# Sums and division of the value products: once per batch, turned by products with a 128x36 selection matrix in place of 128x128 transposes

## The reference, cut to what matters

```python
scores = einsum('bhnd,bhmd->bhnm', q, k) / sqrt(D)
aw = softmax(scores)
topk = 12
kth = top_k(aw, topk)[0][..., -1:]
aws = aw * (aw >= kth)
aws = aws / (aws.sum(-1) + 1e-08)
o_s = einsum('bhnm,bhmd->bhnd', aws, v)
o_l = einsum(qf, kv) / (z + 1e-06)
o = (a * o_s + (1 - a) * o_l).reshape(B, N, C)
return o @ Wproj.T + bproj
```

## Time and profile before

| what | value |
|---|---|
| median of 3 runs | 1333.5 us (1332.71 to 1335.28) |
| span of the profiled execution, first to last instruction | 1331.1 us |
| median less that span | 2.4 us |
| busy share: PE, PEld, DVE, ACT, POOL | 78%, 52%, 95%, 86%, 83% |
| chain that ended last, by engine | DVE 57%, issue 33%, DVEq 6%, all others 3% |
| mean granted TensorE clock over the span | 0.930 |

### The profile page before, as it was taken

One profiled execution on the slowest core, in us unless ns is written; L12 is line 12 of the kernel. 1 busy time (PEld: TensorE's weight loads), 2 busy tenths in 40 slices (PEclk: granted clock), 3 DMA queues, 4 the chain that ended last, 5 costly groups with the idle time before them and its releaser, 6 DMA issues.

```text
span 1331.1 us, 40027 instructions
## 1 busy us (share of the span) xinstructions
PE 1040.0 (78%) x8964; PEld 693.5 (52%) x8964; DVE 1260.1 (95%) x4916; ACT 1138.5 (86%) x3978; POOL 1110.9 (83%) x1458
## 2 busy tenths in 40 slices
PE   3787877778787878877888787777877788787776
PEld 1455555555455555555555455554555555555544
DVE  5799999999999999999999999999999999999995
ACT  3689998989899888989989899888989888898885
POOL 4588898979789888888879889798888888889874
PEclk9989999989899798998989989898998998989998
DMA  2222222112222122221112221112221212221210
GB/s 57 72 59 63 77 77 75 35 57 64 77 76 72 29 64 65 76 77 47 53 53 76 77 76 46 55 57 71 76 76 35 66 53 76 77 76 33 64 49 13
DMA packets 165131, 82.31 MB, mean 62 GB/s; under 512 B 7747, under 2 KB 164933, under 8 KB 164934
## 3 DMA queue, kind: packets, MB, share of 16 engines
q1 hardware_dynamic: 164934, 80.54, 20.9%
HBM read 42.77 MB, written 37.75 MB: 60 GB/s over the span
## 4 chain that ended last, share of the span: by engine, by line
DVE 57%; issue 33%; DVEq 6%; ACT 1%; POOL 1%; PE 1%; DMA 0%; SPq 0%; POOLq 0%
DVE rest L525 21%; DVE top L518 21%; DVE next L531 8%; DVEq L72 5%; DVE drop L615 2%; DVE o_sparse L574 1%; ACT e L719 1%; DVE den L566 1%; DVE k_sum L593 1%; DVE stats L582 0%; PE work_ps L910 0%; PE work_ps L911 0%; DVE x_mv L588 0%; DVE d_max L557 0%; DVE den L571 0%
## 5 line engine op out<-in xcount | busy, mean ns | idle before, releaser
L386 POOL TENSOR_SCALAR below<-e,next 128x256 bf16<-128x256 f32 x768 | 696.1, 922 | 21.5 <-DVE next L531 21.3
L719 ACT ACTIVATE e<-score_ps,drop 128x256 f32<-128x256 f32 x1024 | 472.4, 480 | 108.2 <-DVE drop L615 105.5
L838 PE MATMUL turn_ps<-ident,e 128*128 128x128 f32 x2048 | 429.9, 303 | 10.9 <-ACT kept L685 10.4
L525 DVE MATCH_REPLACE8 rest<-e 128x256 f32<-128x256 f32 x1024 | 413.3, 404 | 0.0
L531 DVE MAX8 next<-rest 128x8 f32<-128x256 f32 x1024 | 407.5, 408 | 0.0
L839 PE MATMUL turn_ps<-minus_huge,below 128*128 128x128 bf16 x2048 | 402.5, 232 | 0.0
L518 DVE MAX8 top<-score_ps 128x8 f32<-128x256 f32 x1024 | 359.4, 410 | 41.8 <-issue 21.7
L838 PEld LDWEIGHTS turn_ps<-ident,e 128*128 128x128 f32 x2048 | 312.2, 152 | 80.9 <-ACT kept L685 17.9
L685 ACT ACTIVATE kept<-turn_ps 128x512 f32<-128x512 f32 x512 | 285.1, 620 | 33.8 <-PE turn_ps L839 14.3
L839 PEld LDWEIGHTS turn_ps<-minus_huge,below 128*128 128x128 bf16 x2048 | 234.5, 115 | 0.0
L719 ACT ACTIVATION_READ_ACCUMULATOR e<-score_ps,drop 128x1 f32 x1024 | 217.1, 212 | 0.0
(11 more groups left out here) (141 smaller groups left out, 1540.6 us busy)
## 6 DMA issues: line engine op xcount, KB each, us to landing
part_slots<-part SPq DMA_DIRECT2D x128, 192.0 KB, 2.3
q_slots<-part_slots SPq DMA_DIRECT2D x64, 256.0 KB, 3.4
k_slots<-part_slots SPq DMA_DIRECT2D x64, 256.0 KB, 4.1
part_slots<-part SPq DMA_DIRECT2D x64, 128.0 KB, 1.9
x_sb<-in_L_attn_x SPq DMA_DIRECT2D x32, 128.0 KB, 3.6
x_res<-in_L_attn_x SPq DMA_DIRECT2D x32, 128.0 KB, 3.7
out_y<-out_sb SPq DMA_DIRECT2D x32, 128.0 KB, 4.2
w_ops<-in_L_ffn_W SPq DMA_DIRECT2D x1, 512.0 KB
```

The costliest lines, as they stand in the source:

```text
L386: nc.gpsimd.tensor_scalar(below[:, r, t, :], e[:, r, t, :], next8[:, r, t, TOPK - 9:TOPK - 8], None, ALU.is_lt).then_inc(s["below_pool"], 1)
L525: nc.vector.match_replace(rest[:, t, :], e8[:, (u_ - 1) % 2, t, :], e[:, (u_ - 1) % RING, t, :], REMOVED).then_inc(s["rest_ready"], 1)
L719: nc.scalar.activation(e[:, u_ % RING, t, :], score_ps[:, u_ % 2, t // 2, t % 2, :], ACT.Exp, bias=drop[:, u_ % 2, t, 0:1], accum_out=z[:, ...
L838: mm(dst, e[:, r, t, keys], ident[:], start=True, stop=False, is_transpose=True)
```

## The change

The transposes of `sums` become products with `heads_of`, a matrix of 128 rows by 4 x 9 columns of zeros and ones that GpSimd makes once at the start: column (j, e) picks partition 32 j + e. A product of a 128x128 block of `oT` (the weights) with it has 36 columns and no gaps, so the two halves of the rows, 2 x 4 x 36 = 288 columns, fit into `pv_ps` (512 columns) together. `sums` now makes all eight products in unit 5, and nothing in unit 7. VectorE works on both halves with one `den` (32 columns in place of 16), one reciprocal and one `o_sparse` (256 columns in place of 128), all in unit 5 at the same places k = 1, 2 and 4. `product` waits in unit 6 for the whole of `o_sparse`, and no longer in unit 0. The arithmetic is the same.

```diff
+        heads_of = sb("heads_of", [P, 4, VA])
...
-        den = sb("den", [P, 2, NT, H])
+        den = sb("den", [P, 2, NT * H])
...
+            nc.gpsimd.memset(heads_of[:], 0.0).then_inc(s["pool_step"], 1)
+            select(heads_of[:], ALU.not_equal, 1.0, 0, [[-VW, 4], [-1, VA]], 1, 7).then_inc(s["pool_const"], 1)
...
-                        pool.wait_ge(s["osp_ready"], NT * (it - 1))
+                        pool.wait_ge(s["osp_ready"], it - 1)
...
-                    if u_ in (5, 7) and 1 <= k <= 4 and exists(it - 1):
-                        t = (u_ - 5) // 2
-                        w = pv_ps[:].rearrange("p (h e) -> p h e", e=VW)
-                        n = 2 * (NT * (it - 1) + t)
+                    if u_ == 5 and 1 <= k <= 4 and exists(it - 1):
+                        w = pv_ps[:, 0:NT * H * VA].rearrange("p (g e) -> p g e", e=VA)
+                        n = 2 * (it - 1)
                         if k == 1:
-                            dve.wait_ge(s["w_turn"], NT * (it - 1) + t + 1)
-                            nc.vector.scalar_tensor_tensor(out=den[:, 0, t], in0=z[:, nxt, t], scalar=SUM_EPS,
-                                                           in1=w[:, :, D], op0=ALU.mult,
+                            dve.wait_ge(s["w_turn"], it)
+                            nc.vector.scalar_tensor_tensor(out=den[:, 0], in0=z[:, nxt].rearrange("p t h -> p (t h)"),
+                                                           scalar=SUM_EPS, in1=w[:, :, D], op0=ALU.mult,
                                                            op1=ALU.add).then_inc(s["den_step"], 1)
                         if k == 2:
                             dve.wait_ge(s["den_step"], n + 1)
-                            nc.vector.reciprocal(den[:, 1, t], den[:, 0, t]).then_inc(s["den_step"], 1)
+                            nc.vector.reciprocal(den[:, 1], den[:, 0]).then_inc(s["den_step"], 1)
                         if k == 4:
                             dve.wait_ge(s["den_step"], n + 2)
-                            nc.vector.tensor_tensor(o_sparse[:, t].rearrange("p (h d) -> p h d", d=D), w[:, :, 0:D],
-                                                    den[:, 1, t].unsqueeze(2).to_broadcast([P, H, D]),
+                            nc.vector.tensor_tensor(o_sparse[:].rearrange("p t (h d) -> p (t h) d", d=D), w[:, :, 0:D],
+                                                    den[:, 1].unsqueeze(2).to_broadcast([P, NT * H, D]),
                                                     ALU.mult).then_inc(s["osp_ready"], 1)
...
-                            wait(act, s["osp_ready"], NT * (it - 1))
+                            wait(act, s["osp_ready"], it - 1)
...
-                            wait(act, s["w_turn"], NT * (it - 1))
+                            wait(act, s["w_turn"], it - 1)
...
-                    if u_ in (0, 6):
-                        wait(pe, s["osp_ready"], NT * (it - 1) + (1 if u_ == 6 else 0))
+                    if u_ == 6:
+                        wait(pe, s["osp_ready"], it)
...
-                def sums(u_):
-
-                    t = (u_ - 5) // 2
-                    pe.wait_ge(s["pv_copied"], QUADS * it + (t if exists(it) else 0))
-                    if t:
-                        pe.wait_ge(s["osp_ready"], NT * (it - 1) + t)
-                    for q in range(QUADS):
-                        last = nc.tensor.transpose(pv_ps[:, q * P:(q + 1) * P],
-                                                   oT[:, nxt, q, t * P:(t + 1) * P], ident[:])
+                def sums():
+
+                    pe.wait_ge(s["pv_copied"], QUADS * it)
+                    for t in range(NT):
+                        for q in range(QUADS):
+                            cols = slice((t * QUADS + q) * 4 * VA, (t * QUADS + q + 1) * 4 * VA)
+                            last = mm(pv_ps[:, cols], oT[:, nxt, q, t * P:(t + 1) * P],
+                                      heads_of[:].rearrange("p j e -> p (j e)"), start=True, stop=True)
                     last.then_inc(s["w_turn"], 1)
...
-                    if u_ in (5, 7) and exists(it - 1):
-                        sums(u_)
+                    if u_ == 5 and exists(it - 1):
+                        sums()
```

More of the change, by code:

```diff
@@ L906, in early @@
                             pe.wait_ge(s["setup_v"], 1)
-                            pe.wait_ge(s["pool_const"], 7)
+                            pe.wait_ge(s["pool_const"], 8)
                         for t in range(NT):
```

## The result

The changed kernel takes **1362.2 us** (median of 4 runs, 1359.7 to 1366.4) against 1333.1 of the kernel before: ratio 1.0235, 95% interval 1.0209 to 1.0262. It is slower, as forecast, but by 29 us where 11 were predicted, and 6 us beyond the end of the range. The profiled execution took 1359.7 us with a span of 1358.0, so the span grew by 26.9.

What follows compares the result with a forecast made beforehand. VectorE, busy for 95% of the span, was taken as the bound. Terms -3.4 + 18.8 - 4 = +11.4 us gave a span of 1342.5, plus 2.4 for the median: 1344.9 us; range 1330 to 1356.

Steps and rivals of the forecast that it cites:

- Sixteen passes at 0.11 us: TensorE's `sums` in unit 5: sixteen passes 0.11 us apart at full clock, ending 1.91 us after the start.
- The term for the last pass: End of `sums` in unit 5: the sixteenth pass, with 36 columns, lasts 0.20 us at full clock.
- the third rival: Faster: weight loads do not set the distance of the passes in unit 5; 1330.1 us, down to 1321; chance 0.2.
- Waits before `den`: VectorE in unit 5 waits for the sixteen passes: 0.07 us at full clock, 1.64 at half, 18.8 in all.
- I keep the counts: Clock in 31 windows of 1.9 us from unit 5's `sums` stays: 17 full, seven partly slow, seven half.
- Part 1: VectorE saves three instructions per batch through the merged `den`, reciprocal and `o_sparse`: 0.11 us per batch, 3.4 us in all.
- The sign that VectorE's busy time would fall by about 12 us: In the changed kernel's profile, VectorE's busy time falls about 12 us, of which only 3.4 are real.
- Part 4: `drop` and the loop's turn: some waiting time is given back, 0.3 us for each of 13 long waits, 4 us.
- Part 3: Work queued behind `den` and the sixteen passes, units 6, 7 and 0, last batch and setup included, costs nothing further.
- `product` in unit 6 and the values: nothing: TensorE's `product` in unit 6 waits for a later `o_sparse`; TensorE is 78% busy, so this costs nothing.
- The fourth rival: TensorE late in unit 6 delays ScalarE's exponentials, so VectorE's `remove` waits: 0.5 us per batch, 1360 us; chance 0.07.
- The rival of few slow stretches: Few slow-clock stretches fall on unit 5's products: only 2.2 us of waits, 1332.3 us, within 0.2%; chance 0.12.

Runs made afterwards that it cites:

- The wide form: The changed kernel with 128 columns in each of the sixteen passes in place of 36; 1354.7 us, ratio 1.017.
- the permutation: The changed kernel with its eight products made as one-pass transposes by a 128x128 permutation matrix; 1336.2 us, ratio 1.0041.
- the earlier copy: The changed kernel with ScalarE's copy of the last quad moved ahead of the exponentials in unit 4; 1338.4 us, ratio 1.0052.

## Why the prediction was right or wrong

**Sixteen passes at 0.11 us: right.** The distance is 0.113 us. The wide form shows that the columns do not set it: behind the first pass, the starts follow each other at 0.112 us with 36 columns and with 128; only the first distance is longer with 128, 0.21 in place of 0.13. That the weight load sets the distance fits, but was not isolated. The term for the last pass (0.20, from 0.8 ns a column) was too small: 0.279 us, since 36 columns last as long as 128 do (0.273 in the earlier trace rows). It made 0.07 us of wait into 0.16, 1.5 us in 17 batches. The Trainium skill (TensorE: Matmul & The Clock Gate, LDWEIGHTS) gives an estimate of 107 ns for such a load, and the distance of 113 agrees. Its section Back-to-back issue gap, whose 25 ns the third rival took, gives them for an isolated gap and says that in a stream of loads and matmuls both set the spacing; here it was 113 ns.

**Waits before `den`: right in sum, 18.6 against 18.8, and partly by luck.** The make-up differed: 2.8, 6.7 and 9.0 us for full, partly slow and half clock, predicted 1.3, 6.0 and 11.5. A longer wait in each batch was made up by five windows at half clock in place of seven. "I keep the counts" held for the 1.9 us of the passes (17, nine, five). It did not hold for what stands behind them: over 6 us the slow time rose from 54.6 to 91.3.

**Part 1, VectorE saves 3.4 us: near, but spent.** Without the wait the medians fall by 5.6 us. About 1 of that is taken back, since the short value load behind the reciprocal stands once per batch in place of twice, so 4.5 are saved. With the wait 4.4 of it is lost again, 3.2 because the instruction behind a waiting `den` starts 0.21 us after it and not 0.09. The prediction reckoned the wait as its bare length. The sign that VectorE's busy time would fall by about 12 us failed: it rose by 4.8. Even with the permutation it falls only by 2.1 (1260.1 to 1258.0), since durations that overlap are counted once. The prediction also held the fixed cost that the Trainium skill gives for an instruction reading PSUM (VectorE: DVE Perf Modes, The TRN2 errata) against a distance. Beside the duration of `o_sparse`, 0.26 us in the earlier trace rows, it fits: 128 elements and that cost come to an estimate of 0.26 us.

**Part 4, "given back, 4 us": wrong in sign.** This is the step that failed most. Nothing was given back: `drop`, which was to fall by 4 us, rose by 3.6. The kernel with the permutation, where `den` hardly waits, is the measure. The span of the change is 23.5 us longer than its, and the waits (19.2) and VectorE's higher medians (4.3) are all of that; `drop` (+2.5), `rest` (-2.2) and `next` (-0.7) cancel. Why the others did not catch up in the wait, as they do at the loop's turn, is not shown. That TensorE, for which they wait, is itself late (the 42.4 us before `v_aug`) fits, but it does not reach `rest`: VectorE's idle time there is 2.1 us with these 42.4, and 4.1 with the permutation and its 7.1. With its row of ScalarE busy for the whole window the prediction had the argument against a give-back in hand and still took a fifth of it.

**Part 3, nothing queued behind costs anything: wrong.** `rest` and `next` come 5.1 us later in the change and 8.0 with the permutation, so this is a cost of the merging itself, for which the sum had no term. The last batch, costed at nothing, lost 1.0 us. "`product` in unit 6 and the values: nothing" is contradicted by the 42.4 us that ScalarE is idle before `v_aug`, 8.5 before; what VectorE pays for them was not isolated. The fourth rival, a second wait by way of ScalarE, had 0.07, and that its 1360 us is nearest to the result is luck: the wait that it names, `rest` for the exponentials, grew by 1.1 us and not by 15.

In numbers: the span was forecast to grow by 11.4 and grew by 26.9. Of the 15.5 between them, 7.6 are part 4 (-4 predicted, +3.6 measured in `drop`), 5.1 are `rest` and `next` (+2.3 and +2.8, no term in the sum), 2.1 is part 1 (-3.4 predicted, -1.3 measured), 1.0 the end of the run, -0.2 the waits, -0.2 all else. Beyond that the measured median stands 4.2 us over the span, and 2.4 were reckoned.

**The rival of few slow stretches** would have needed fewer than the 14 of 31 that came. That of **faster** fell with the distance.

## What to carry to other kernels

Where one engine bounds a kernel without a gap, instructions saved on it are worth less than one later signal from another: here 5.6 us saved stood against 23 us of waits and of restarts behind them. Before such a trade, count the new passes against the slack at half clock too, add about 0.1 us for each wait on top of its length, and count nothing as given back unless a run shows it. Merging work can also cost something where nothing waits, here 9 us against the 5.6 by which the medians fell. An f32 product with few columns costs two passes as long as full ones; a one-pass transpose with a permutation does the same turn in half the time.

## What the runs showed of the hardware that was not expected

- A plain f32 pass with 36 columns lasts 278 to 279 ns at full clock, one with 128 columns 274 to 275, a transpose with 128 272 to 273. Behind the first pass of a round the distance is 0.112 us with either. Few columns save next to nothing here.
- An instruction behind one that waited for a semaphore starts later: 0.21 us after `den` in 27 of the 32 batches of the change, 0.09 to 0.10 in 27 of 32 with the earlier copy. Outside the loop it was 0.12 in four batches with a wait.
- The same eight passes in a round come with a slow clock in 23 of 31 windows of 6 us with 36 columns and in 11 or 14 with 128, though the mean clock of the run does not change (0.931, 0.936, 0.931). What the clock goes by was not isolated.
- The cost of a round depends on what stands behind it: products in unit 5 alone cost 8 us, those of unit 7 19 more on top, and as many passes of transposes in both 1 us.
